# Inverse softmax sums spread by a VectorE block transpose and two DMAs through DRAM instead of GpSimd, TensorE and ScalarE

## Chip, cores and metric

One NeuronCore of a Trainium2 chip runs the whole program. The metric is the device time of one execution in microseconds (us). The kernel before takes 1790.45 us (median of three runs, 1790.11 to 1791.4).

## What is computed

Input and output are 2 x 2048 tokens of 256 features, fp32. The first part is an attention with 16 heads of 16 and an MLP; the second is two layers, each a local attention with 8 heads of 64 and a gated MLP. The change is in the attention of these two layers, called B here:

```python
w = n // WINDOW                                   # windows of 128 tokens
bk, bv = (look_around(bk), look_around(bv))       # keys and values of this window and the one before
sim = jnp.einsum('bhwid,bhwjd->bhwij', bq, bk)
sim = jnp.where(mask, -jnp.finfo(sim.dtype).max, sim)
attn = jax.nn.softmax(sim, axis=-1)
out = jnp.einsum('bhwij,bhwjd->bhwid', attn, bv)
...
x = x + o @ wo
```

The division of the softmax is done late: the kernel forms exp(sim - max) @ v without it and multiplies the result by 1 / sum, once per head and query.

## The kernel before

The tokens are cut into 32 chunks of 128 (`NCH`), a chunk being one window of one batch. A B attention is one loop of software-pipelined steps `s`, written out by hand for each engine. In step `s` TensorE does, in this order: `scores(s)` (L851, two rounds of four heads), `values(s-1)` (L890), `spread_inverse(s-1)` (L911), `project_k(s+2)`, `transpose_probs(s,0)` (L877), `project_q(s+2)`, `transpose_x(s+3)`, `transpose_probs(s,1)`, `transpose_rotated(s+1)`, `out_project(s-2)` (L923), `project_v(s+2)` (L830). Each engine runs its list in order and waits on semaphores; nothing is reordered.

VectorE does in step `s`: `maxima(s)` (L1330, eight masked maxima out of PSUM), `rotate_q(s+1)`, `scale_o(s-1)` (L1360, `O` times `b_inv_t`), `copy_probs(s,0)` (L1347, recorded at L1450), `scale_rotated(s+1)` (L1311), `norms(s+2,1)`, `copy_probs(s,1)`, `norms(s+2,0)` (L1286, with the small L1295), `invert_sums(s)` (L1354), `h_low(s+3)` (L1281), `k_t_low`, `q_t_low` (L1320, L1325), `add_residual(s-2)` (L1367). ScalarE does the exponentials (L1828, which also give `row_sum`), copies out of PSUM, among them `copy_spread(s-1)` (L1848) between its two rounds of exponentials. GpSimd does `o_low`, in the steps 5, 7, ... 19 a piece of splitting the MLP weights (L1138), `inverse_norms` (L2066), `tables` (L2045), `rotate_k(s+2)` (L2056), `widen_inverse(s)` (L2076). SyncE issues all DMAs (`sp_attention`, L388).

The sums stand with queries on partitions and heads on columns (`row_sum`, 128 x 8). The output `O` of `values` stands with features on partitions (two heads of 64 rows in each of four 128-column tiles) and queries on columns. So the inverse must be turned and repeated 64 times: VectorE inverts (128 x 8), GpSimd repeats each column 64 times (`b_inv_wide`, 128 x 512), TensorE turns four 128 x 128 blocks into PSUM bank W2 (bank 1), ScalarE copies W2 to `b_inv_t`, and VectorE multiplies.

Bank W2 has three users in a step: the spread, the transposed input (`transpose_x(s+3)`, read by ScalarE's `h_high` and VectorE's `h_low`) and `project_v(s+2)`, read by ScalarE's `copy_v`. `project_v(n)` waits at L836 for `h_lo` to have reached `min(n + 2, NCH)`, that is, for `h_low(s+3)` of the same step. The last chunks of an attention overlap the first groups of the MLP behind it: at `s == NCH - 2` SyncE issues that MLP's first loads (`sp_mlp(..., opening=True)`, L493), and at `s == NCH - 1` VectorE interleaves the MLP's normalisation with `scale_o(30)` and `invert_sums(31)`.

Of the kernel before, what the change touches and what calls it, by code (L numbers as in the profile page):

```python
# [6 lines left out]
F32 = mybir.dt.float32  # L7
# [6 lines left out]
P = 128  # L14
# [142 lines left out]
def build(nc, io):  # L157
# [5 lines left out]
    x_mid_sh = nc.dram_tensor("x_mid_sh", (TOK + P, P), F32, kind="Internal").ap()  # L163

    ctx = ExitStack()
    with ctx:
# [20 lines left out]
        minus_half = sbuf("minus_half", [P, 16])  # L187
        vec_a = sbuf("vec_a", [P, 16])
# [42 lines left out]
        b_inv, b_inv_wide = sbuf("b_inv", [P, 8], at=b_ctx), sbuf("b_inv_wide", [P, 512], at=b_ctx)  # L231
        b_inv_t = sbuf("b_inv_t", [P, 512], at=b_ctx)
# [64 lines left out]
        def sems(prefix, names):  # L297
# [11 lines left out]
            inv_ready inv_wide inv_spread r_copied o_scaled o_hi o_lo wo_ready y_ready""")  # L309
# [78 lines left out]
        def sp_attention(sp, layer, opening=False):  # L388

            S, g0 = SB, layer * NCH  # L390
# [385 lines left out]
        def pe_attention(pe, layer, opening=False):  # L776
# [10 lines left out]
            def transpose_x(n):  # L787
# [7 lines left out]
                if n > 3:  # L795
                    pe.wait_ge(S["v_copied"], g0 + n - 1)
                    pe.wait_ge(S["r_copied"], g0 + n - 3)
# [32 lines left out]
            def project_v(n):  # L830
# [6 lines left out]
                if n >= 3:  # L837
                    pe.wait_ge(S["r_copied"], g0 + n - 2)
# [72 lines left out]
            def spread_inverse(n):  # L911

                pe.wait_ge(S["inv_wide"], g0 + n + 1)
                pe.wait_ge(S["v_copied"], g0 + min(n + 3, NCH))
                if n == NCH - 2:
                    pe.wait_ge(S["y_ready"], g0 + NCH - 3)
                if n == NCH - 1:
                    pe.wait_ge(S["r_copied"], g0 + n)
# [33 lines left out]
            for s in b_steps():  # L952
# [320 lines left out]
        def dve_attention(v, layer, opening=False):  # L1273
# [80 lines left out]
            def invert_sums(n):  # L1354
                v.wait_ge(S["exp_ready"], 2 * (g0 + n) + 2)
# [960 lines left out]
```

## Time and profile before

| | us |
|---|---|
| median of three runs | 1790.45 |
| profiled execution, first to last instruction | 1791.1 |
| of it, first B attention (571 to 978) | 407 |
| second B attention (1180 to 1592) | 412 |

The page of the profile gives for the whole span: TensorE busy 97%, VectorE 83%, ScalarE 67%, GpSimd 60%; the DMA queue that SyncE fills takes 20.5% of 16 engines' time. In the views, times are microseconds from the start of the span; PE is TensorE (matmul), PEld its weight loads, DVE VectorE, ACT ScalarE, POOL GpSimd, SPq SyncE's DMA issues. A number in square brackets at the end of a row is idle time of the engine before that instruction, with what ended it. Where a row has xN, it joins N instructions of one kind.

### The profile page before, as it was taken

How to read it: one execution, taken by the hardware profiler on the slowest of the kernel's cores; microseconds unless marked ns; L12 is line 12 of the kernel's file. 1: busy time of each engine (PE TensorE's matmuls, PEld its weight loads, DVE VectorE, ACT ScalarE, POOL GpSimd, SP SyncE). 2: the span in 40 equal slices, each digit the busy share in tenths (PEclk: the TensorE clock that was granted, in tenths of full speed). 3: DMA queues.
4: the chain of work that ended last, by engine and by line, in shares of the span. 5: the costliest groups of instructions: out<-in, count | busy, mean ns of one | idle time of the engine just before them, and what ended most of it. 6: DMA issues, size and time to landing. Idle time of an engine off the chain costs nothing.

```text
span 1791.1 us, 43798 instructions
## 1 busy us (share of the span) xinstructions
PE 1731.2 (97%) x15424; PEld 1496.0 (84%) x15424; DVE 1494.1 (83%) x3797; ACT 1197.5 (67%) x3088; POOL 1080.0 (60%) x1060
## 2 busy tenths in 40 slices
PE   6999999999999999999999999989999999999997
PEld 4778777789998888888887888878888888888886
DVE  6888988868878898888987678789898898967776
ACT  6999988854445787877876334358787877743332
POOL 3676556534434778778773455377878777634343
PEclk9999999999999999999999999999999999999999
DMA  3111211032322111111112434331111111131221
GB/s 107 38 37 38 67 44 31 26 107 75 108 63 99 48 41 54 44 52 51 44 43 71 147 105 126 100 103 41 52 44 55 41 54 47 31 102 56 82 82 36
DMA packets 139812, 116.03 MB, mean 65 GB/s; under 512 B 10584, under 2 KB 138848, under 8 KB 138848
## 3 DMA queue, kind: packets, MB, share of 16 engines
q1 hardware_dynamic: 139616, 113.53, 20.5%
q8 instruction: 109, 1.79, 0.4%
q14 instruction: 87, 0.71, 0.1%
HBM read 75.74 MB, written 37.75 MB: 63 GB/s over the span
## 4 chain that ended last, share of the span: by engine, by line
PE 84%; DVE 9%; ACT 3%; issue 3%; POOL 0%; DMA 0%; SPq 0%; DVEq 0%; POOLq 0%; ACTq 0%
PE psum L567 17%; PE psum L569 17%; PE psum L568 17%; PE psum L906 6%; PE psum L874 5%; PE psum L887 5%; PE psum L682 3%; PE psum L664 3%; PE psum L848 3%; ACT a_probs L1718 2%; PE psum L920 2%; PE psum L617 1%; DVE a_neg_max L1211 1%; DVE psum L1209 1%; PE psum L654 1%
## 5 line engine op out<-in xcount | busy, mean ns | idle before, releaser
L1837 ACT ACTIVATE b_probs<-masked,neg_max 128x256 f32<-128x256 f32 (+1 forms) x512 | 250.6, 494 | 124.3 <-DVE neg_max L1343 124.3
L1343 DVE CUSTOM_DVE_ANT_0 masked<-psum,mask 128x256 f32<-128x256 f32 (+1 forms) x512 | 177.3, 412 | 75.9 <-PE psum L874 75.9
L567 PE MATMUL psum<-wa_hi,b_h_hi 128*128 128x512 f32 (+1 forms) x576 | 233.8, 406 | 6.9 <-DVE wa_lo L1138 3.9
L568 PE MATMUL psum<-wa_lo,b_h_hi 128*128 128x512 f32 (+1 forms) x576 | 214.0, 372 | 0.0
L569 PE MATMUL psum<-wa_hi,b_h_lo 128*128 128x512 f32 (+1 forms) x576 | 214.0, 372 | 0.0
L567 PE MATMUL psum<-g_h_hi,wm_hi 128*128 128x512 f32 (+1 forms) x480 | 190.5, 397 | 2.7 <-POOL g_h_lo L2121 1.6
L2070 POOL TENSOR_TENSOR g_in<-g_in,minus_half 128x16 f32<-128x16 f32 x64 | 188.2, 2940 | 4.5 <-DVE g_in L1295 4.5
L568 PE MATMUL psum<-g_h_lo,wm_hi 128*128 128x512 f32 (+1 forms) x480 | 189.3, 394 | 0.0
L569 PE MATMUL psum<-g_h_hi,wm_lo 128*128 128x512 f32 (+1 forms) x480 | 189.2, 394 | 0.0
L1458 POOL TENSOR_TENSOR g_in<-g_z,g_in 128x512 f32<-128x512 f32 x62 | 79.8, 1287 | 143.4 <-DVE g_in L1289 138.2
L567 PE MATMUL psum<-wm_hi,u_hi 128*128 128x256 f32 x576 | 164.3, 285 | 0.1
L1931 ACT ACTIVATE gate<-psum,vec_b 128x512 f32<-128x512 f32 x96 | 66.1, 688 | 146.4 <-PE psum L569 146.3
L569 PE MATMUL psum<-wm_hi,u_lo 128*128 128x256 f32 x576 | 162.7, 283 | 0.0
L568 PE MATMUL psum<-wm_lo,u_hi 128*128 128x256 f32 x576 | 162.5, 282 | 0.0
L1718 ACT ACTIVATE a_probs<-psum,a_neg_max 128x128 f32<-128x128 f32 x512 | 148.5, 394 | 5.0 <-DVE a_neg_max L1211 4.9
L2008 POOL TENSOR_SCALAR_AFFINE_SELECT p_before<-p_now 128x512 f32<-128x512 f32 x120 | 76.6, 638 | 119.6 <-ACT p_now L1728 119.6
L887 PE MATMUL psum<-ident,b_probs 128*128 128x128 f32 x992 | 129.8, 273 | 3.7 <-ACT b_probs L1837 3.7
L569 PEld LDWEIGHTS psum<-wa_hi,b_h_lo 128*128 128x128 f32 x576 | 109.4, 190 | 19.9
L567 PEld LDWEIGHTS psum<-wa_hi,b_h_hi 128*128 128x128 f32 x576 | 109.7, 190 | 18.9 <-DVE wa_lo L1138 4.3
L887 PEld LDWEIGHTS psum<-ident,b_probs 128*128 128x128 f32 x992 | 113.0, 140 | 14.7 <-ACT b_probs L1837 6.7
L906 PE MATMUL psum<-b_pt,v_tok 128*64 128x128 f32 x1984 | 123.4, 277 | 0.0
L2117 POOL TENSOR_TENSOR g_rstd<-g_ve,minus_half 128x4 f32<-128x4 f32 x24 | 25.1, 1046 | 161.8 <-DVE g_ve L1487 161.8
(169 smaller groups left out, 5644.0 us busy)
## 6 DMA issues: line engine op xcount, KB each, us to landing
x_mid<-y_out SPq DMA_DIRECT2D x96, 128.0 KB, 1.7
rope_in<-in_rope SPq DMA_DIRECT2D x64, 128.0 KB, 2.2
x_res<-x_state SPq DMA_DIRECT2D x64, 128.0 KB, 2.2
g_in<-x_mid SPq DMA_DIRECT2D x32, 256.0 KB, 3.8
g_old<-x_state SPq DMA_DIRECT2D x16, 512.0 KB, 4.0
out_x<-g_fin SPq DMA_DIRECT2D x15, 512.0 KB, 2.9
w_raw<-in_w_mlp_b SPq DMA_DIRECT2D x2, 2154.0 KB, 8.8
x_in<-in_x SPq DMA_DIRECT2D x32, 128.0 KB, 2.2
```

What stands on the lines that cost most here:

```text
L567: nc.tensor.matmul(out, a_hi, b_hi, start=first, stop=False)
L568: nc.tensor.matmul(out, a_hi, b_lo, start=False, stop=False)
L569: return nc.tensor.matmul(out, a_lo, b_hi, start=False, stop=last)
L874: mm = nc.tensor.matmul(outs[b], q[rows, t, :], k[rows, t, at, :], start=first, stop=last)
L887: mm = nc.tensor.transpose(bank[4 + 2 * r + k // 2][:, at:at + P], b_probs[:, r, k, half, :], ident[:])
L906: mm = nc.tensor.matmul(O[rows, t * P:t * P + P], v_tok[m % U][:, h * 64:h * 64 + 64], b_pt[:, r, 2 * j + b, half, :], start=(m == blocks[ ...
L1343: ins = nc.vector.tensor_tensor_reduce(out[:, at], src[:, at], (mask if now else mask0)[:, at], -1.0, BIG, ALU.add, ALU.min, neg_max[:, r, ...
L1458: engine.tensor_tensor(cos_part[i][:].rearrange("p (h d) -> p h d", d=64), x, table(2 * i, 0, 64), ALU.mult).then_inc(done, 1)
L1718: ins = nc.scalar.activation(a_probs[:, i % 2, k, :], bank[4 + 2 * (i % 2) + b][:, at:at + P], ACT.Exp, bias=a_neg_max[:, n % 2, r, k:k + ...
L1837: ins = nc.scalar.activation(out, src, ACT.Exp, bias=neg_max[:, r, k:k + 1], scale=-1.0, accum_out=row_sum[:, n % 2, 4 * r + k:4 * r + k + 1])
L2008: nc.gpsimd.affine_select(before, now, [[0, 4], [-1, P]], ALU.is_ge, 0.0, base=-1, channel_multiplier=1)
L2070: nc.gpsimd.tensor_tensor(rnorm[:], norm2c[:], minus_half[:], ALU.pow).then_inc(S["rnorm_ready"], 1)
```

## The change

`spread_inverse`, `copy_spread` and `widen_inverse` go, with their semaphores and the waits on them. `b_inv` becomes 128 x 32, its columns 8 to 31 holding ones. VectorE, after the reciprocal, turns `b_inv` in 32 x 32 blocks into `b_inv_turned`: partition 32 g + h holds head h of the queries 32 g to 32 g + 31. SyncE stores that (128 rows of 128 bytes) to a DRAM tensor with heads on rows and 128 queries on columns, waits until it has landed, and issues two reads, each of which fills 64 partitions with the same four rows (256 pieces of 512 bytes each), into one half of a doubled `b_inv_t`. `scale_o` waits for these reads. `invert_sums(s)` moves forward in VectorE's order, from behind `norms(s+2,0)` to behind `scale_rotated(s+1)`. On SyncE the three DMAs of chunk `s` stand at the head of step `s`, ahead of the store of `y(s-2)`; in step 0 behind the last store of the layer before; in step 30 behind the first loads of the MLP.

```diff
@@ sp_attention
+            def inverse_of(n):
+                return inverse_rows[(n % 2) * 32:(n % 2) * 32 + 32, :]
+            def store_inverse(n):
+                sp.wait_ge(S["inv_turned"], g0 + n + 1)
+                if g0 + n >= 2:
+                    sp.wait_ge(S[f"inv_spread{n % 2}"], 32 * ((g0 + n) // 2))
+                sp.dma_start(inverse_of(n).rearrange("h (g q) -> g h q", q=32), b_inv_turned[:]).then_inc(S["inv_stored"], 16)
+            def spread_inverse(n):
+                sp.wait_ge(S["inv_stored"], 16 * (g0 + n + 1))
+                if g0 + n >= 2:
+                    sp.wait_ge(S["o_scaled"], g0 + n - 1)
+                for b in range(2):
+                    src = inverse_of(n)[0:c.NH, :].rearrange("(t b) q -> b t q", b=2)[b:b + 1, :, :].to_broadcast([c.DH, 4, P])
+                    sp.dma_start(b_inv_t[b * c.DH:(b + 1) * c.DH, n % 2, :, :], src).then_inc(S[f"inv_spread{n % 2}"], 16)
...
                 if s == NCH - 2:
                     sp_mlp(sp, MLP_B, MB, layer, opening=True)
+                if b_chunk(s) and s > 0:
+                    store_inverse(s)
+                    spread_inverse(s)
                 if b_chunk(s - 2):
                     store(s - 2)
...
                     sp_mlp(sp, *mlp_behind(layer), None if layer == 0 else layer - 1, opening="last")
+                    store_inverse(0)
+                    spread_inverse(0)
@@ pe_attention
                     pe.wait_ge(S["v_copied"], g0 + n - 1)
-                    pe.wait_ge(S["r_copied"], g0 + n - 3)
...
-                if n >= 3:
-                    pe.wait_ge(S["r_copied"], g0 + n - 2)
...
-            def spread_inverse(n):
-                pe.wait_ge(S["inv_wide"], g0 + n + 1)
-                pe.wait_ge(S["v_copied"], g0 + min(n + 3, NCH))
...
-                for t in range(4):
-                    mm = nc.tensor.transpose(W2[:, t * P:t * P + P], b_inv_wide[:, t * P:t * P + P], ident[:])
-                mm.then_inc(S["inv_spread"], 1)
...
-                    pe.wait_ge(S["r_copied"], g0 + NCH - 2)
+                    pe.wait_ge(S["v_copied"], g0 + NCH)
...
                     values(s - 1, 1)
-                    spread_inverse(s - 1)
@@ dve_attention
             def invert_sums(n):
                 v.wait_ge(S["exp_ready"], 2 * (g0 + n) + 2)
+                nc.vector.reciprocal(b_inv[:, 0:c.NH], row_sum[:, n % 2, :]).then_inc(S["inv_ready"], 1)
+                v.wait_ge(S["inv_ready"], g0 + n + 1)
                 if g0 + n > 0:
-                    v.wait_ge(S["inv_wide"], g0 + n)
-                nc.vector.reciprocal(b_inv[:], row_sum[:, n % 2, :]).then_inc(S["inv_ready"], 1)
+                    v.wait_ge(S["inv_stored"], 16 * (g0 + n))
+                nc.vector.transpose(b_inv_turned[:], b_inv[:]).then_inc(S["inv_turned"], 1)
 
             def scale_o(n):
-                v.wait_ge(S["r_copied"], g0 + n + 1)
+                v.wait_ge(S[f"inv_spread{n % 2}"], 32 * ((g0 + n) // 2) + 32)
...
                     scale_rotated(s + 1)
+                if b_chunk(s) and s != NCH - 1:
+                    invert_sums(s)
                 if s == NCH - 2:
                     add_residual(s - 2)
...
                     norms(s + 2, 0)
-                if b_chunk(s) and s != NCH - 1:
-                    invert_sums(s)
@@ act_attention
-            def copy_spread(n):
-                a.wait_ge(S["inv_spread"], g0 + n + 1)
-                if g0 + n > 0:
-                    a.wait_ge(S["o_scaled"], g0 + n)
-                nc.scalar.activation(b_inv_t[:], W2[:], ACT.Copy).then_inc(S["r_copied"], 1)
@@ pool_attention
-            def widen_inverse(n):
-                pool.wait_ge(S["inv_ready"], g0 + n + 1)
-                if n == 0:
-                    pool.wait_ge(zero_rows_stored, layer * 32 + 16)
...
-                nc.gpsimd.tensor_copy(b_inv_wide[:].rearrange("p (h d) -> p h d", d=64),
-                                      b_inv[:].unsqueeze(2).to_broadcast([P, 8, 64])).then_inc(S["inv_wide"], 1)
```

## Rows read from the trace of the kernel before

**Rows 1.** The page, part 4: the chain that ended last, by engine.

```profile
PE 84%; DVE 9%; ACT 3%; issue 3%; POOL 0%; DMA 0%; SPq 0%; DVEq 0%; POOLq 0%; ACTq 0%
```

**Rows 2.** Busy time by engine: a step with weights split, then a plain one.

```profile
core 0: us, PE busy (x) PEld busy (x) DVE busy (x) ACT busy (x) POOL busy (x), PEclk, DMA share, GB/s
684.59:697.20 12.61, 12.61 (x118) 11.14 (x118) 11.38 (x33) 9.91 (x28) 10.62 (x10) 1.00 0.16 49
722.42:735.01 12.59, 12.59 (x119) 11.12 (x118) 11.28 (x33) 10.45 (x29) 9.43 (x9) 1.00 0.15 48
```

**Rows 3.** The chain that ended last, in the plain step: start, length, engine, line.

```profile
725.96 0.59 PE psum L920 x4
```

**Rows 4.** Timeline, plain step, VectorE: start, length, line, operation, output<-input, shapes.

```profile
723.39 0.42 DVE L1343 CUSTOM_DVE_ANT_0 masked<-psum,mask 128x256 f32<-128x256 f32 x1 [1.17 <-PE psum L874]
...
728.15 0.68 DVE L1365 TENSOR_TENSOR b_o<-psum,b_inv_t 128x512 f32<-128x512 f32 x1
728.86 0.69 DVE L1450 COPY b_pt<-psum 128x512 f32<-128x512 f32 x1
729.46 1.28 DVE L1318 TENSOR_TENSOR g_in<-g_in 128x512 f32<-128x512 f32 x2
730.66 0.68 DVE L1289 TENSOR_REDUCE g_in<-k_sq 128x8 f32<-128x512 f32 x1
...
731.95 0.68 DVE L1289 TENSOR_REDUCE g_in<-q_sq 128x8 f32<-128x512 f32 x1
732.65 0.17 DVE L1295 TENSOR_SCALAR g_in<-g_in 128x16 f32<-128x16 f32 x1
732.75 0.19 DVE L1358 RECIPROCAL b_inv<-row_sum 128x8 f32<-128x8 f32 x1
732.86 0.37 DVE L1283 TENSOR_TENSOR b_h_lo<-psum,b_h_hi 128x256 fp32r<-128x256 f32 x1
```

**Rows 5.** Timeline, plain step, TensorE: first scores, V projection's load, next first scores.

```profile
722.37 0.39 PE L874 MATMUL psum<-k_t_hi,q_t_hi 64*128 64x256 f32 x2
...
733.34 0.19 PEld L567 LDWEIGHTS psum<-wa_hi,b_h_hi 128*128 128x128 f32 x1
...
734.94 0.39 PE L874 MATMUL psum<-k_t_hi,q_t_hi 64*128 64x256 f32 x2
```

**Rows 6.** Timeline, plain step, GpSimd: the K rotation's first product.

```profile
731.51 1.29 POOL L1458 TENSOR_TENSOR g_in<-g_z,g_in 128x512 f32<-128x512 f32 x1 [2.41 <-DVE g_in L1289]
```

**Rows 7.** Timeline, step with weights split: GpSimd, VectorE and TensorE's load.

```profile
691.10 0.75 POOL L2053 TENSOR_TENSOR g_in<-rope_in,rope_scale 128x256 f32<-128x256 f32 x1
...
691.61 1.39 DVE L1318 TENSOR_TENSOR g_in<-g_in 128x512 f32<-128x512 f32 x2
...
695.11 0.36 DVE L1283 TENSOR_TENSOR b_h_lo<-psum,b_h_hi 128x256 fp32r<-128x256 f32 x1
...
695.53 0.19 PEld L567 LDWEIGHTS psum<-wa_hi,b_h_hi 128*128 128x128 f32 x1
```

**Rows 8.** Timeline, VectorE, first chunk of the second batch.

```profile
778.69 0.42 DVE L1449 COPY b_pt<-psum 128x256 f32<-128x256 f32 x1 [0.51 <-PE psum L887]
```

**Rows 9.** The page, part 6: DMA issues, KB each, median us to landing.

```profile
x_mid_sh<-y_out SPq DMA_DIRECT2D x64, 64.0 KB, 1.7
g_in<-x_mid_sh SPq DMA_DIRECT2D x16, 256.0 KB, 3.5
```

**Rows 10.** Ends of both layers: SyncE's first y store and its landing, `scale_o(30)`.

```profile
960.90 0.75 SPq L405 DMA_DIRECT2D x_mid<-y_out  x1
DMA to landing us min/median/max: 1.7/1.7/3.8
...
965.55 0.68 DVE L1365 TENSOR_TENSOR b_o<-psum,b_inv_t 128x512 f32<-128x512 f32 x1
...
1570.38 0.50 SPq L405 DMA_DIRECT2D x_mid<-y_out  x1
...
1576.43 0.68 DVE L1365 TENSOR_TENSOR b_o<-psum,b_inv_t 128x512 f32<-128x512 f32 x1
```

**Rows 11.** Busy time, second layer, scores of chunk 31; PEclk is the granted clock.

```profile
1569.00:1572.00 3.00, 3.00 (x26) 2.78 (x28) 1.39 (x9) 0.00 (x0) 0.88 (x1) 0.50 0.94 248
```

More of the change, by code:

```diff
@@ L163, in build @@
     x_mid_sh = nc.dram_tensor("x_mid_sh", (TOK + P, P), F32, kind="Internal").ap()
+    inverse_rows = nc.dram_tensor("inverse_rows", (2 * 32, P), F32, kind="Internal").ap()
     ctx = ExitStack()
@@ L187, in build @@
         minus_half = sbuf("minus_half", [P, 16])
+        b_inv = sbuf("b_inv", [P, 32])
+        b_inv_turned = sbuf("b_inv_turned", [P, 32])
         vec_a = sbuf("vec_a", [P, 16])
@@ L230, in build @@
         row_sum = sbuf("row_sum", [P, 2, 8], at=b_ctx)
-        b_inv, b_inv_wide = sbuf("b_inv", [P, 8], at=b_ctx), sbuf("b_inv_wide", [P, 512], at=b_ctx)
-        b_inv_t = sbuf("b_inv_t", [P, 512], at=b_ctx)
+        b_inv_t = sbuf("b_inv_t", [P, 2, 4, P], at=b_ctx)
         b_o = sbuf("b_o", [P, 512], at=b_ctx)
@@ L308, in build @@
             scores_ready max_ready exp_ready pt_ready pt_act pt_dve pv_done
-            inv_ready inv_wide inv_spread r_copied o_scaled o_hi o_lo wo_ready y_ready""")
+            inv_ready inv_turned inv_stored inv_spread0 inv_spread1 o_scaled o_hi o_lo wo_ready y_ready""")
         mlp_names = """load0 load1 old0 old1 store out_store params stats aggr var rstd z_ready xt_ready h32_ready h_hi h_lo h_lo_pool
@@ L388, in sp_attention @@
         def sp_attention(sp, layer, opening=False):
-            S, g0 = SB, layer * NCH
+            c, S, g0 = ATT_B, SB, layer * NCH
             def load(n):
@@ L909, in values @@
                 mm.then_inc(S["pv_done"], 1)
-            def spread_inverse(n):
-                pe.wait_ge(S["inv_wide"], g0 + n + 1)
-                pe.wait_ge(S["v_copied"], g0 + min(n + 3, NCH))
[L915 to L918, printed above, removed]
-                for t in range(4):
-                    mm = nc.tensor.transpose(W2[:, t * P:t * P + P], b_inv_wide[:, t * P:t * P + P], ident[:])
-                mm.then_inc(S["inv_spread"], 1)
             def out_project(n):
                 if n == NCH - 4:
-                    pe.wait_ge(S["r_copied"], g0 + NCH - 2)
+                    pe.wait_ge(S["v_copied"], g0 + NCH)
                 elif n == NCH - 3:
@@ L1364, in scale_o @@
                     v.wait_ge(S["o_lo"], g0 + n)
-                nc.vector.tensor_tensor(b_o[:], O[:], b_inv_t[:], ALU.mult).then_inc(S["o_scaled"], 1)
+                nc.vector.tensor_tensor(b_o[:].rearrange("p (t q) -> p t q", q=P), O[:].rearrange("p (t q) -> p t q", q=P),
+                                        b_inv_t[:, n % 2, :, :], ALU.mult).then_inc(S["o_scaled"], 1)
             def add_residual(n):
@@ L1647, in _ @@
             nc.vector.memset(big[:], -MASKED)
+            nc.vector.memset(b_inv[:], 1.0)
             nc.vector.memset(minus_half[:], -0.5).then_inc(consts_set, 1)
@@ L1880, in act_attention @@
                     exponentials(s, 0)
-                if b_chunk(s - 1):
-                    copy_spread(s - 1)
                 if b_chunk(s):
@@ L2074, in o_low @@
                 nc.gpsimd.tensor_tensor(b_o_lo[:], b_o[:], b_o_hi[:].bitcast(F32), ALU.subtract).then_inc(S["o_lo"], 1)
-            def widen_inverse(n):
-                pool.wait_ge(S["inv_ready"], g0 + n + 1)
-                if n == 0:
-                    pool.wait_ge(zero_rows_stored, layer * 32 + 16)
-                if g0 + n > 0:
-                    pool.wait_ge(S["inv_spread"], g0 + n)
-                nc.gpsimd.tensor_copy(b_inv_wide[:].rearrange("p (h d) -> p h d", d=64),
-                                      b_inv[:].unsqueeze(2).to_broadcast([P, 8, 64])).then_inc(S["inv_wide"], 1)
             if opening:
@@ L2109, in pool_attention @@
                     rotate_k(s + 2)
-                if b_chunk(s):
-                    widen_inverse(s)
             pool.wait_ge(S["y_ready"], g0 + NCH)
```

## Prediction

> **What bounds the kernel now.** I read the chain that ended last first: 84% of it lies on TensorE and 9% on VectorE [rows 1]. The change only touches the two later attentions, so the next view is one step (one chunk of 128 tokens) of them. TensorE is busy for all of such a step, 12.61 us in a step in which GpSimd also splits weights and 12.59 us in one in which it doesn't (a plain step) [rows 2]. The four transposes that spread the inverse sums are a piece of 0.59 us of that chain [rows 3]. Taken alone this says: 0.59 us less per step, 64 times. But the chain shows only which engine was last, not how late the next one was. So I laid VectorE's order beside TensorE's in a plain step [rows 4, 5].
>
> The link that matters is bank W2. `project_v(s+2)` writes it and waits until VectorE's `h_low(s+3)` (L1283) has read it. In the plain step `h_low` ends at 732.86 + 0.37 = 733.23, and TensorE loads the first weights of `project_v` at 733.34 [rows 4, 5]: 0.11 us of slack. In the other kind `h_low` ends at 695.11 + 0.36 = 695.47 and the load comes at 695.53 [rows 7]: there TensorE waits for it already, and 0.06 us is the price of the handover. From that load to the next scores are 734.94 - 733.34 = 1.60 us, and from scores to the first maximum 723.39 - 722.37 = 1.02 us [rows 4, 5]. So there is a second ring, VectorE from the first maximum to `h_low`, then `project_v`, then scores, and it is as long as TensorE's own. The removed transposes aren't in it.
>
> **The change, part by part, inside that ring.** Removed from TensorE: 0.59 us. It would reach `project_v` 0.59 us sooner and find `h_low` not done; what hides the gain is that ring. ScalarE's copy of the spread and GpSimd's widening are gone from engines that the ring doesn't wait for, GpSimd in one place excepted (below); that frees them and moves nothing.
>
> What VectorE gains: it waits once for TensorE inside the ring. `scale_o` to the first `copy_probs` takes 728.86 - 728.15 = 0.71 us, while the same kind of operation passes on after 729.46 - 728.86 = 0.60 [rows 4]; 0.10 us goes away.
>
> What VectorE gets: the reciprocal now has a follower that waits for it. Before, it cost the pitch 732.86 - 732.75 = 0.11 us. Now it costs its full 0.19 us plus some 0.03 for the handover to itself (L1289, 0.68 us from 731.95, has its dependant at 732.65, 0.02 after its end) [rows 4]: 0.22 us. The 32x32 turn over 128x32 is in no row. Its pitch is bounded below by zero (wholly overlapped; a gain is excluded for the instruction itself) and above by that of a 128x256 operation, 0.29 us (0.37 us less the 0.08 that neighbours overlap). Nearest is the 128x8 reciprocal with 0.19; I take 0.21 us of duration, 0.13 of pitch. Sum 0.22 + 0.13 = 0.35 us, and 0.11 is taken from its old place: 0.24 net. Both now stand behind `scale_rotated`, ahead of `norms` and `copy_probs(s,1)`. They wait for ScalarE's exponentials, which are over before that; queued behind them are the norms, on which GpSimd's K rotation waits, the second copy, for which `values` has time until the next step, and `h_low`, which has none.
>
> One more link: VectorE's tiny L1295 begins at 732.65 and ends at 732.82, and GpSimd's K rotation ends at 731.51 + 1.29 = 732.80 [rows 4, 6]. The Trainium skill (SBUF — State Buffer, section "Who interferes with whom") says that a VectorE tensor_scalar in a two-port mode and a GpSimd instruction exclude each other for a whole instruction. By the row I take the moment as fixed at 2.09 us after the K norms start (730.66 to 732.75), since the rotation starts behind those norms; without such a tie it would be 2.01, and the plain steps would give 3.0 us less in all.
>
> Plain step: first maximum to K norms 730.66 - 723.39 = 7.27, less 0.10, plus 0.35 is 7.52; plus 2.09 and 0.37 gives 9.98 for the end of `h_low`; plus 0.06, 1.60 and 1.02 gives 12.66 us, against 734.94 - 722.37 = 12.57 now: +0.09. There are 19 such steps per layer: +3.4 us for two layers. Step with weights split: the same terms (-0.10, +0.24), and `scale_rotated` loses 0.11 (1.39 us for two against 1.28), because GpSimd's L2053 at 691.10, lasting 0.75, which overlaps it, comes earlier once the widening is gone [rows 4, 7]: +0.03, 7 per layer, +0.4 us. In the half-size step of the second batch's first chunk VectorE waits 0.51 us for TensorE [rows 8], and in the step of chunk 29 there is no `h_low` to wait for. The gain of each lies between nothing and 0.59; I count 0.45 (most of the wait shown) and 0.4, once per layer: -1.7 us in all. In the first step of a layer the scores of chunk 1 wait for VectorE's `q_t_low`, behind the pair: +0.24 twice, +0.5. Steady part: +2.6 us.
>
> **The round trip through DRAM.** The rows for SyncE's transfers give 1.7 us from issue to landing for 64 KB stored, and for loads in 512-byte rows up to 3.5 us [rows 9]. The new chain in a plain step: turned at 7.52 behind the first maximum, stored at about 9.4, two loads issued 0.5 apart, the second landed by 9.5 + 0.5 + 3.5 = 13.5. `scale_o` asks for it in the next step at 12.66 + 4.76 = 17.4 (728.15 - 723.39 = 4.76 into the step). 3.9 us of cover; hidden. SyncE's own queue: the y store, residual and x loads are pushed behind by three issues, which their next users, a step or more later, don't feel.
>
> Where the cover is gone is the end of a layer. There SyncE first issues the loads of the next MLP and only then this store: it would leave at about 960.90, where now a y store leaves that lands 3.8 us later [rows 10]. So 964.7, plus 0.1, 0.5 and 3.0 for the loads behind the MLP's is 968.3, while `scale_o(30)` stands at 965.55: about 2.7 us. In the second layer 1570.38 + 3.8 + 3.6 = 1577.8 against 1576.43: 1.4 us. VectorE's order behind it leads straight into the MLP's first chunk, so these are paid. The turn itself is in that stretch too (0.25 a layer), and chunk 31's trip is late by some 0.35. Ends: 2.7 + 1.4 + 0.5 + 0.7 = +5.3 us. The bound below is none (the transfers land in time), the one above twice that.
>
> The Trainium skill (SBUF — State Buffer, "The DMA setup-cost knee") puts a fixed 2 us on every transfer. By it alone the trip of chunk 30 would land at 965.5 and 1575.0, cost nothing, and the sum would be 4.1 us less; the row of a store issued in just that place, 3.8 us, speaks against it.
>
> Sum: 2.6 + 5.3 = +7.9 us. The profiled execution spans 1791.1 us and the median of the three timed runs is 1790.45, so the one may be put on the other: 1798.3 us.
>
> **Rivals.**
> - TensorE stays the bound (the other side). If `h_low` does not hold `project_v` back, every full step falls to 12.0 us: 58 times 0.59 is -34, with the ends +5: about 1762. It decides from the point where `h_low` ends at least 0.59 us ahead of TensorE; the rows show 0.11 and 0. For it speaks only TensorE's share. Chance 0.08.
> - The same ring, but the pair on VectorE costs almost nothing beyond the old reciprocal, or the end of the layer is covered. With 0 instead of 0.24 the 52 steps give 12 us less than forecast; half of that, or the ends at zero, puts it near 1792: no measurable change. Chance 0.23.
> - The ends cost more: TensorE idles longer, and its clock falls. In the second layer the granted clock was 0.50 for the three microseconds from 1569 [rows 11], after TensorE had waited for VectorE; two more such stretches cost about 1.3 us each, and a loaded queue may add 2 us per layer: 1806. A turn as dear as a 128x256 operation ends there too. Chance 0.17.
> - The trip is late in every step: it must take over 9.9 us from the turn to landing, and then each microsecond costs some 60 us. Against it speaks the cover of 3.9 us. Chance 0.04, 1850 and more.
> - Forecast, 1792 to 1804: 0.48. That the removed instructions stay is excluded by the diff.
>
> The range reaches down to a free turn and up to the third rival: 1787 to 1811. About 0.2% (3.6 us) is what a measurement of this kernel can tell from none. Slower 0.66, same 0.22, faster 0.12.
>
> **What would show it.** Right: plain steps of 12.6 to 12.7 us, with TensorE's busy time near 12.0 in them and its idle time ahead of `project_v`, released by L1283's line; `scale_o` waiting for a transfer only for chunk 30 (and slightly 31) of a layer. Wrong: steps of 12.0 to 12.3 (the ring is looser), a turn over 0.4 us, or `scale_o` waiting in each step.

## The result, and the profile after

The changed kernel takes 1807.91 us in the median of four runs (1807.04 to 1810.35), the kernel before 1790.93 beside it (1790.11 to 1791.54). The ratio is 1.0096, with a 95% interval of 1.0084 to 1.0107: 17 us slower. The forecast was 1798.3 us, +7.9 us. The direction and the range hold, but the cost is more than twice what was forecast.

The profiled execution of the changed kernel spans 1807.0 us, 15.9 more than that of before. Its page, busy time by engine and then the chain that ended last:

```profile
PE 1722.9 (95%) x15168; PEld 1475.8 (82%) x15168; DVE 1503.3 (83%) x3862; ACT 1170.2 (65%) x3024; POOL 1043.5 (58%) x996
...
PE 56%; DVE 30%; issue 8%; ACT 3%; DMA 2%; SPq 1%; DVEq 0%; POOL 0%; POOLq 0%; ACTq 0%
```

In [rows 1] the same line read TensorE 84% and VectorE 9%. TensorE was relieved, and a part of the chain went over to VectorE (9% to 30%). The plain step that answers [rows 2], from scores to scores (columns as there):

```profile
712.44:725.11 12.67, 12.45 (x113) 10.76 (x113) 11.41 (x34) 9.52 (x27) 10.11 (x9) 1.00 0.25 70
```

The step is 12.67 us long, as forecast (12.66), and TensorE is now idle for 0.22 us of it. VectorE's timeline over the same kind of step answers [rows 4]:

```profile
718.22 0.68 DVE L1378 TENSOR_TENSOR b_o<-psum,b_inv_t 128x512 f32<-128x512 f32 x1
718.82 0.68 DVE L1464 COPY b_pt<-psum 128x512 f32<-128x512 f32 x1
719.41 1.28 DVE L1329 TENSOR_TENSOR g_in<-g_in 128x512 f32<-128x512 f32 x2
720.62 0.19 DVE L1367 RECIPROCAL b_inv<-row_sum 128x8 f32<-128x8 f32 x1
720.84 0.21 DVE L1371 STREAM_TRANSPOSE b_inv_turned<-b_inv 128x32 f32<-128x32 f32 x1
720.98 0.64 DVE L1300 TENSOR_REDUCE g_in<-k_sq 128x8 f32<-128x512 f32 x1
...
722.85 0.26 DVE L1306 TENSOR_SCALAR g_in<-g_in 128x16 f32<-128x16 f32 x1
723.03 0.41 DVE L1294 TENSOR_TENSOR b_h_lo<-psum,b_h_hi 128x256 fp32r<-128x256 f32 x1
...
724.56 0.41 DVE L1385 TENSOR_TENSOR y_out<-psum,x_res 128x256 f32<-128x256 f32 x1
726.12 0.42 DVE L1354 CUSTOM_DVE_ANT_0 masked<-psum,mask 128x256 f32<-128x256 f32 x1 [1.16 <-PE psum L898]
```

Three of the forecast's prices can be read here. The turn lasts 0.21 us (0.21 was taken). The reciprocal and the turn (the pair, in what follows) together move VectorE on by 720.98 - 720.62 = 0.36 us (0.35 was taken). The scaling passes on to the copy after 0.60 us, so the 0.10 us of waiting are gone. TensorE in the same step, answering [rows 5]:

```profile
723.49 0.50 PE L594 MATMUL psum<-wa_hi,b_h_hi 128*128 128x512 f32 x1 [0.22 <-DVE b_h_lo L1294]
...
725.11 0.39 PE L898 MATMUL psum<-k_t_hi,q_t_hi 64*128 64x256 f32 x2
```

**Where the 15.9 us lie.** Both kernels scale the values once per chunk (L1365 before, L1378 after), so its 64 starts mark the same point of the work in each. The differences after - before of the times between these starts are:

| stretch | before, us | after, us | difference | forecast |
|---|---|---|---|---|
| layer 1, up to chunk 1 | 602.17 | 604.14 | +1.97 | +0.25 |
| layer 1, chunks 2 to 29 | 352.05 | 353.42 | +1.37 | +1.05 |
| layer 1, chunks 30 and 31 | 18.14 | 23.94 | +5.80 | 3.3 |
| between, up to layer 2's chunk 1 | 239.61 | 239.68 | +0.07 | +0.25 |
| layer 2, chunks 2 to 29 | 351.72 | 353.51 | +1.79 | +1.05 |
| layer 2, chunks 30 and 31 | 19.30 | 24.66 | +5.36 | 2.0 |
| behind it | 208.11 | 207.65 | -0.46 | 0 |

So the steady steps cost about what was said (3.2 us against 2.1 for these chunks). The surprise is at the ends: 11.2 us against 5.3. The start of the first layer adds 1.7 us more. Here is the end of layer 1 in the changed kernel, first VectorE and SyncE's queue (SPq):

```profile
960.19 0.21 DVE L1371 STREAM_TRANSPOSE b_inv_turned<-b_inv 128x32 f32<-128x32 f32 x1
...
963.70 0.51 SPq L494 DMA_DIRECT2D g_in<-x_mid  x1
964.31 0.57 SPq L433 DMA_DIRECT2D inverse_rows<-b_inv_turned  x1
968.90 1.26 SPq L442 DMA_DIRECT2D b_inv_t<-inverse_rows  x2
...
972.66 0.69 DVE L1378 TENSOR_TENSOR b_o<-psum,b_inv_t 128x512 f32<-128x512 f32 x1 [3.69 <-DMA b_inv_t<-inverse_rows]
973.27 2.32 DVE L1506 TENSOR_SCALAR g_z<-g_in,g_mv,g_rstd 128x256 f32<-128x256 f32 x4
975.51 0.19 DVE L1367 RECIPROCAL b_inv<-row_sum 128x8 f32<-128x8 f32 x1
...
981.50 0.69 DVE L1378 TENSOR_TENSOR b_o<-psum,b_inv_t 128x512 f32<-128x512 f32 x1 [0.37 <-DMA b_inv_t<-inverse_rows]
```

Chunk 30's inverses are turned at 960.40, but SyncE is issuing the MLP's loads until 964.2. The store goes out at 964.31, and the reads that wait for its landing are issued 4.6 us later. Its answering row in [rows 10] was 965.55. Behind the scaling that waits stand g_z (the normalised input of the MLP) and the turn of chunk 31, so chunk 31's trip starts only at 975.9. In layer 2 the wait is as long (3.87 us at 1589.97), but the kernel before itself is 1.4 us slower there than in layer 1 (12.74 us up to chunk 30 against 11.33), with the clock at 0.50 for a stretch [rows 11]; the changed kernel's execution has the clock at 1.00 there, so the difference of that end, +5.36, comes out smaller by that much. TensorE and the granted clock (PEclk, third number from the end of a window) in that place:

```profile
975.74 1.94 PE L1035 MATMUL psum<-ident,g_z 128*128 128x128 f32 x8 [5.21 <-DVE g_z L1506]
...
971.00:974.00 3.00, 0.00 (x0) 0.00 (x0) 1.34 (x4) 0.77 (x2) 0.00 (x0) 1.00 0.56 168
974.00:977.00 3.00, 1.26 (x6) 1.29 (x7) 2.97 (x6) 0.02 (x1) 1.34 (x1) 0.60 0.00 0
977.00:980.00 3.00, 3.00 (x26) 2.67 (x26) 1.64 (x3) 0.65 (x1) 0.00 (x0) 0.50 0.16 42
```

TensorE idles for 5.21 us, and the clock falls to the lower of its two levels (1.2 of 2.4 GHz) when it starts again.

### The profile page after: what moved, and what is told of

Its sections match the earlier page's. It is cut to its first block, busy times and chain, and to the rows that moved or that the text cites. A ratio compares the mean times of both kernels' runs of the same rounds, so it can differ in the third digit from the quotient of the medians.

```text
span 1807.0 us, 43288 instructions
## 1 busy us (share of the span) xinstructions
PE 1722.9 (95%) x15168; PEld 1475.8 (82%) x15168; DVE 1503.3 (83%) x3862; ACT 1170.2 (65%) x3024; POOL 1043.5 (58%) x996
## 4 chain that ended last, share of the span: by engine, by line
PE 56%; DVE 30%; issue 8%; ACT 3%; DMA 2%; SPq 1%; DVEq 0%; POOL 0%; POOLq 0%; ACTq 0%
PE psum L594 14%; PE psum L596 13%; PE psum L595 13%; DVE masked L1354 7%; DVE g_in L1329 4%; PE psum L709 3%; PE psum L898 3%; PE psum L691 3%; DVE b_pt L1464 3%; DVE g_in L1300 2%; ACT a_probs L1733 2%; DVE g_in L1472 2%; PE psum L644 1%; DVE a_neg_max L1222 1%; DVE psum L1220 1%
## 5 line engine op out<-in xcount | busy, mean ns | idle before, releaser
L594 PE MATMUL psum<-wa_hi,b_h_hi 128*128 128x512 f32 (+1 forms) x576 | 239.9, 416 | 19.1 <-DVE b_h_lo L1294 14.7
L595 PEld LDWEIGHTS psum<-wa_lo,b_h_hi 128*128 128x128 f32 x576 | 110.4, 192 | 11.0
```

What stands on the lines that cost most here:

```text
L594: nc.tensor.matmul(out, a_hi, b_hi, start=first, stop=False)
L595: nc.tensor.matmul(out, a_hi, b_lo, start=False, stop=False)
```

## The experiments

For each run these numbers count: the ratio to the kernel before on the same chip, and from the trace of one execution the plain step and the two ends (chunks 30 and 31 together, layer 1 / layer 2), both as times between starts of the scaling. The kernels of the rows "no turn", "before, no transposes" and "chunk 30 without its wait" leave out a part of the work (the turn, the transposes, chunk 30's inverses), to price it.

| kernel | median, us | ratio and 95% interval | plain step | ends |
|---|---|---|---|---|
| before | 1790.93 | 1 | 12.57, 12.63 | 18.14 / 19.30 |
| changed | 1807.91 | 1.0096 (1.0084 to 1.0107) | 12.67 | 23.94 / 24.66 |
| TensorE's transposes back | 1814.04 | 1.0138 (1.0121 to 1.0154) | 12.80 | 24.19 / 24.33 |
| turn behind h_low | 1806.17 | 1.0095 (1.0078 to 1.0112) | 12.68 | 25.02 / 25.10 |
| MLP loads behind | 1804.22 | 1.0080 (1.0063 to 1.0097) | 12.68 | 23.17 / 23.09 |
| no turn | 1791.73 | 1.0003 (0.9993 to 1.0012) | 12.42 | 24.21 / 24.58 |
| before, no transposes | 1789.06 | 0.9987 (0.9977 to 0.9996) | 12.57 | 18.14 / 18.23 |
| norms behind | 1790.63 | 0.9991 (0.9982 to 1.0001) | 12.36, 12.44 | 24.52 / 25.01 |
| before, norms behind | 1786.35 | 0.9974 (0.9965 to 0.9984) | 12.57 | 18.14 / 19.29 |
| chunk 30 without its wait | 1797.12 | 1.0031 (1.0021 to 1.0041) | 12.68 | 20.52 / 20.57 |
| TensorE kept busy | 1805.49 | 1.0074 (1.0056 to 1.0091) | 12.68 | 25.13 / 25.65 |
| g_z first | 1799.88 | 1.0047 (1.0030 to 1.0064) | 12.68 | 20.40 / 20.37 |
| ends mended | 1797.56 | 1.0033 (1.0020 to 1.0046) | 12.68 | 19.80 / 20.10 |
| all of it | 1777.53 | 0.9922 (0.9905 to 0.9938) | 12.36, 12.44 | 19.75 / 19.91 |

**TensorE's transposes put back.** Does TensorE's time count in a step?

```
# TensorE, behind values(s - 1), chunks 0 to 28
+ pe.wait_ge(S["v_copied"], g0 + n + 3)
+ for t in range(4):
+     nc.tensor.transpose(W2[:, t * P:t * P + P], ident[:], ident[:])
```

> The changed kernel, with TensorE given its four transposes of each of chunks 0 to 28 back (58 chunks in all, four 128x128 transposes into bank W2 behind the values, of data that nothing uses); nobody waits for their result but the next projection into the bank, on TensorE itself. Theory of the ring (VectorE's first maximum, h_low, the projection of the values, the scores): in a steady step TensorE waits for h_low longer than these 0.59 us last, so the time stays at that of the changed kernel, 1807 to 1809 us. Rival, that TensorE's own time sets a step: 58 x 0.59 = 34 us more, about 1842 us.

The result lies between the two: 12.80 us a step, +0.13 and neither 0 nor +0.59. The rival falls, and the ring as I had it (nobody waits for these transposes) is not whole either. The trace shows where most of the 0.13 goes in. VectorE's first copy of probabilities follows the scaling after 0.71 us here and after 0.60 in the changed kernel. The transposes of probabilities that it reads stand behind the four added ones on TensorE:

```profile
717.04 0.69 DVE L1385 TENSOR_TENSOR b_o<-psum,b_inv_t 128x512 f32<-128x512 f32 x1
717.75 0.69 DVE L1471 COPY b_pt<-psum 128x512 f32<-128x512 f32 x1
```

**The turn moved behind h_low.** By my ring the pair leaves the path.

```
# VectorE
- invert_sums(s)            # behind scale_rotated
  ...
  h_low(s + 3)
+ invert_sums(s)
  k_t_low(s + 1)
```

> The changed kernel, with VectorE's reciprocal and turn of a step moved from ahead of h_low to behind it (ahead of k_t_low). Ring: the two instructions (0.36 us by their start-to-start times in the trace) leave the chain that holds a step, about 52 steady steps are shorter by up to that, at most 18.7 us less, near 1789 us; the steady step falls from 12.67 to about 12.31 us. What could eat it: the values in DRAM are stored later by half a us, and scale_o then waits for its DMA, which gives a part back. Rival, that VectorE's order does not matter: 1808 us and a step of 12.67 us.

The step stayed at 12.68 us, so the ring ending in `h_low` fell as the thing that alone sets the step. TensorE's `project_v` no longer waits, but now the scores do (TensorE and VectorE of this run):

```profile
722.13 0.42 DVE L1385 TENSOR_TENSOR y_out<-psum,x_res 128x256 f32<-128x256 f32 x1
...
722.69 0.39 PE L898 MATMUL psum<-k_t_hi,q_t_hi 64*128 64x256 f32 x2 [0.28 <-DVE y_out L1385]
...
723.71 0.42 DVE L1354 CUSTOM_DVE_ANT_0 masked<-psum,mask 128x256 f32<-128x256 f32 x1 [1.16 <-PE psum L898]
```

The scores wait (`y_ready`, in the kernel's code) for the residual sum `y_out`, the last thing that VectorE does in a step, since they write the bank that it reads. From its start to the scores are 0.56 us here. In the changed kernel it is 725.11 - 724.56 = 0.55, and in the kernel before 722.37 [rows 5] less the 721.81 of this row of before:

```profile
721.81 0.41 DVE L1371 TENSOR_TENSOR y_out<-psum,x_res 128x256 f32<-128x256 f32 x1
```

That is 0.56 again. So all of VectorE's order lies in the ring: first maximum, everything up to `y_out`, the scores, and again the first maximum, with VectorE's only idle time, 1.16 us, at the handover. It makes no difference where in that order an instruction stands. My arm over `h_low` and `project_v` is as long to within 0.1 us, which is why its number was right: with the pair's 0.36 us taken out of it, TensorE is idle for 0.28 us ahead of the scores, and with the pair in it, in the changed kernel, for none.

**The turn left out.**

```
# VectorE, in invert_sums
- nc.vector.transpose(b_inv_turned[:], b_inv[:])
# SyncE, in store_inverse
- sp.wait_ge(S["inv_turned"], g0 + n + 1)
+ sp.wait_ge(S["inv_ready"], g0 + n + 1)
```

> The changed kernel without VectorE's turn of 32x32 blocks: the store reads a buffer that holds ones, so the output is not scaled by the inverse sums, and all else is as it was. Prices the turn alone: by the ring about 0.21 to 0.24 us less in each of 52 steady steps, 11 to 12.5 us less in all and some more at the ends, 1794 to 1797 us; the steady step falls from 12.67 to 12.43 us. Rival, that VectorE has the time free: 1807 us.

The step is 12.42 us (12.43 said), the time 1791.73 us, 2 us below what was expected, and the reciprocal passes on after 0.11 us where it was 0.36:

```profile
717.55 0.20 DVE L1367 RECIPROCAL b_inv<-row_sum 128x8 f32<-128x8 f32 x1
717.66 0.64 DVE L1300 TENSOR_REDUCE g_in<-k_sq 128x8 f32<-128x512 f32 x1
```

The turn costs 0.25 us a step, 13 us in 52 steps, of the 16.7 us between the ratios 1.0096 and 1.0003: 0.14 of it is its own (720.84 to 720.98), and 0.11 the reciprocal's, which now has a follower that waits for it. In the changed kernel most of these 13 us don't show as a loss, because VectorE was relieved elsewhere in the step (0.10 us of waiting at the copy, and 0.11 in `scale_rotated` in the steps in which GpSimd splits weights). Without the turn that relief pays for the dearer ends, and the time is that of the kernel before. Taken together with the run before: moving the turn brings nothing, leaving it out brings its full price. That is the mark of a ring that holds a whole engine.

**The kernel before without TensorE's transposes.** The same question there.

```
# TensorE, in spread_inverse
- for t in range(4):
-     mm = nc.tensor.transpose(W2[:, t * P:t * P + P], b_inv_wide[:, t * P:t * P + P], ident[:])
- mm.then_inc(S["inv_spread"], 1)
+ pe.sem_inc(S["inv_spread"], 1)
# ScalarE
- nc.scalar.activation(b_inv_t[:], W2[:], ACT.Copy)
+ nc.scalar.activation(b_inv_t[:], b_inv_wide[:], ACT.Copy)
```

> The kernel before, without TensorE's four transposes of the repeated inverses (ScalarE copies the block in SBUF, not turned; the scaling uses wrong factors). The run with VectorE's turn moved showed that the step did not care where on VectorE it stood, and in both kernels the scores start 0.56 us after the residual sum starts. Theory of VectorE's whole line: all of VectorE's work of a step, and the 1.16 us from its last instruction over the scores to the first maximum, hold a step, in the kernel before too; there a copy of probabilities waits some 0.09 us for TensorE, and that alone goes: 50 steps x 0.09 to 0.12 = 5 to 6 us less, 1785 to 1787 us. Rival, that the kernel before is held by TensorE's stream: 58 x 0.59 = 34 us less, 1757 us.

It gives 2.3 us less by the ratio, and the steps are 12.57 us throughout, where before they were 12.57 and 12.63. It is the direction of the whole line, at half its size. The rival (1757) is out: TensorE's stream alone did not hold the kernel before, although the chain of waits put 84% on it.

**VectorE's Q norms moved into its idle time.** If the whole line is the ring, the cure is to fill the 1.16 us.

```
# VectorE
- norms(s + 2, 0)           # ahead of h_low
  ...
  add_residual(s - 2)
+ norms(s + 2, 0)
```

> The changed kernel, with VectorE's sum of squares of Q and the clamp behind it (0.60 + 0.27 us in the trace) moved from ahead of h_low to behind the residual sum, into the 1.16 us in which VectorE waits for the scores. Theory of the whole line: the step falls by up to 0.86 us until TensorE holds it; TensorE's own instructions of a step are 12.57 - 0.59 = 11.98 us and small waits of 0.1 to 0.2: 12.0 to 12.2 us a step, 52 x 0.47 to 0.67 = 24 to 35 us less, 1773 to 1784 us. Rival, that GpSimd's reciprocal root (2.9 us) comes late by it and its wait takes the place: 1800 to 1808 us.

> The same move in the kernel before. Theory: VectorE is relieved here too, but TensorE's instructions fill 12.57 us of a step of 12.58 to 12.63, so almost nothing comes of it: 0 to 5 us less, 1786 to 1791 us. The difference to the changed kernel with the same move is what TensorE's 0.59 us are worth once VectorE does not hold the step. Rival, that VectorE alone held it: 24 to 35 us less, as in the changed kernel.

In the changed kernel the step falls from 12.67 to 12.36 and 12.44 us, and the time by 1.0096 - 0.9991, 19 us. In the kernel before it stays at 12.57, and the 4.7 us less in all lie in the trace mostly in the stretches up to each layer's chunk 1 (2.1 us each). So both engines held the kernel before at one length, TensorE at 12.57 (this run) and VectorE at 12.57 (the run without transposes). The direction is as expected for both, but the first missed its size for two reasons. VectorE's clamp, 0.26 us long in the changed kernel, takes 1.09 here, until GpSimd's K rotation ends (722.05 + 1.32 = 723.37), and the first maximum is held until then:

```profile
722.05 1.32 POOL L2071 TENSOR_TENSOR g_in<-g_in,k_sq 128x512 f32<-128x512 f32 x1
...
722.31 1.09 DVE L1306 TENSOR_SCALAR g_in<-g_in 128x16 f32<-128x16 f32 x1
723.31 0.41 DVE L1354 CUSTOM_DVE_ANT_0 masked<-psum,mask 128x256 f32<-128x256 f32 x1
```

The Trainium skill (SBUF — State Buffer, "Who interferes with whom") calls the port pair that VectorE and GpSimd share an exclusive lock. By that rule a clamp that starts under a GpSimd instruction is held until that one ends, and these rows agree (the clamp ends at 723.40). The second reason is that TensorE's floor is not 11.98 us. By starts, the four transposes hold up the next projection in the kernel before by 0.41 us, not 0.59, which was the length of a piece up to its modelled end [rows 3]:

```profile
725.89 0.66 PE L920 MATMUL psum<-ident,b_inv_wide 128*128 128x128 f32 x4
726.30 0.48 PE L567 MATMUL psum<-wa_hi,b_h_hi 128*128 128x512 f32 x1
```

The floor without the transposes is then 12.57 - 0.41 = 12.16 us. No run takes the two reasons apart.

**The ends: SyncE's order.**

```
# SyncE, s == NCH - 2
- sp_mlp(sp, MLP_B, MB, layer, opening=True)
  store_inverse(s); spread_inverse(s)
+ sp_mlp(sp, MLP_B, MB, layer, opening=True)
```

> The changed kernel, with SyncE's opening loads of the next MLP issued behind the store and the reads of chunk 30's inverses, not ahead of them, in both layers. Theory of the ends: chunk 30's store waited 0.6 us to be issued and landed after 4.6 us because the loads were in the queues ahead of it; without them its trip is about 3 us shorter, and the clock falls less: 3 to 5 us less at each end, 1798 to 1801 us in all. Rival, that the loads then come late and their own wait takes its place, or that another wait holds the end: 1806 to 1808 us.

A third of it came: the ratio is 1.0080, 2.9 us less, and the trace has 2.3 of it at the ends, where 6 to 10 were expected. Chunk 30's trip is over in time, but now VectorE waits for the MLP's input, which is the rival:

```profile
970.67 1.40 DVE L1494 BATCH_NORM_STATS2 g_stats<-g_in 128x6 f32<-128x256 f32 x4 [3.35 <-DMA g_in<-x_mid]
```

Chunk 31 still comes late: 8.40 and 8.98 us after chunk 30, which here waits for nothing, against 6.81 and 6.56 in the kernel before.

**Chunk 30 without its wait.**

```
# VectorE, scale_o, n == NCH - 2
- v.wait_ge(S[f"inv_spread{n % 2}"], ...)
- in1 = b_inv_t[:, n % 2, :, :]
+ in1 = ident[:].unsqueeze(1).to_broadcast([P, 4, P])
```

> The changed kernel, where the scaling of chunk 30 in both layers takes a constant matrix (the identity, four times over) in place of the inverses and does not wait for their trip; the trip is made all the same. Prices that wait alone with what hangs on it. Theory, that the trip and the fall of TensorE's clock behind it make the ends dear: chunk 30 comes 3.7 and 2.5 us earlier, and the second half of the end, which runs at the lower clock, 1 to 2 us in each layer: 8 to 11 us less, 1797 to 1800 us. Rival, that only the wait counts and the clock falls anyway: 6 us less, 1802 us.

The ratio is 1.0031, 11.6 us below that of the changed kernel. In the trace the ends are 20.52 and 20.57 us, 3.4 and 4.1 shorter, and neither has a fall of the clock. What stays over the kernel before (+2.4 in layer 1) is chunk 31's own wait:

```profile
967.79 0.21 DVE L1371 STREAM_TRANSPOSE b_inv_turned<-b_inv 128x32 f32<-128x32 f32 x1
...
974.62 0.69 DVE L1385 TENSOR_TENSOR b_o<-psum,b_inv_t 128x512 f32<-128x512 f32 x1 [2.20 <-DMA b_inv_t<-inverse_rows]
```

From the end of the turn to the scaling are 974.62 - 968.00 = 6.6 us. The kernel before has far less room at this place; from the work behind its reciprocal to the scaling of chunk 31 are 4.6 us:

```profile
967.79 1.24 DVE L1450 COPY b_pt<-psum 128x512 f32<-128x512 f32 x2
...
972.36 0.68 DVE L1365 TENSOR_TENSOR b_o<-psum,b_inv_t 128x512 f32<-128x512 f32 x1
```

So chunk 31's trip is uncovered whether chunk 30 waits or not: chunk 31 comes 9.20 and 9.24 us after chunk 30 here, 8.84 and 9.38 in the changed kernel.

The ends explain 7.5 of the 11.6 us. The rest lies in other stretches. In the one profiled execution, 15.0 us shorter than that of the changed kernel, the MLP between the layers is 1.9 us shorter and the start 3.5; the clock fell at other places in the two, and I can't tie this to the edit.

**The clock.** Forty transposes of the identity on TensorE while it waits for g_z.

```
# TensorE, s == NCH - 1, ahead of the transposes of g_z
+ for t in range(40):
+     nc.tensor.transpose(bank[MLP_B.FIRST_Z[0]][:, t % 4 * P:t % 4 * P + P], ident[:], ident[:])
```

> The changed kernel, with 40 transposes of the identity added on TensorE at the end of each layer (into a bank that is written anew right behind them), in the 5.2 us in which TensorE waits there for g_z: about 40 x 0.11 = 4.4 us of work that nobody needs. Prices the fall of the granted clock that follows that wait (0.60 and 0.50 in the windows behind it, the transposes of g_z, the values and VectorE's g_z slower). Theory, that the idle wait brings the fall: the clock stays at 1.00 behind it, and 2 to 3 us of each end come back, 4 to 6 us less in all, 1802 to 1804 us. Rival, that the clock falls all the same, or that the transposes are in the way: 1807 to 1811 us.

In layer 1 the clock stayed at 1.00 where it was 0.60 and 0.50:

```profile
974.00:977.00 3.00, 2.33 (x32) 2.16 (x34) 2.97 (x7) 0.00 (x0) 0.47 (x1) 1.00 0.04 5
977.00:980.00 3.00, 2.28 (x25) 1.91 (x20) 1.27 (x2) 1.06 (x1) 1.24 (x1) 1.00 0.17 49
...
980.67 0.47 PE L594 MATMUL psum<-g_h_hi,wm_hi 128*128 128x512 f32 x1 [1.39 <-POOL g_h_lo L2119]
...
981.69 0.69 DVE L1380 TENSOR_TENSOR b_o<-psum,b_inv_t 128x512 f32<-128x512 f32 x1 [2.29 <-DMA b_inv_t<-inverse_rows]
```

From chunk 30's scaling to the MLP's first matmul are 980.67 - 971.68 = 8.99 us, against 982.82 - 972.66 = 10.16 in the changed kernel. In this pair of executions the fall costs 1.2 us up to that matmul, not 2 to 3. In layer 2 the clock still fell (to 0.69). By the ratios, 1.0074 against 1.0096, the run is 3.9 us faster (1805.49 us, 1802 to 1804 expected), but their intervals overlap, so the size is not settled. Chunk 31 gained nothing (10.01 us behind chunk 30 instead of 8.84): what stands ahead of it came earlier, its trip did not, and it waits 2.29 us for it instead of 0.37. SyncE took 2.17 us to issue its two reads instead of 1.26. The slow g_z was not the clock's doing either: it takes 2.33 us here too. The last of its four instructions lasts 1351 ns (tile g_z in the changed kernel) and runs while GpSimd makes `b_o_lo`:

```profile
974.10 1.34 POOL L2081 TENSOR_TENSOR b_o_lo<-b_o,b_o_hi 128x512 fp32r<-128x512 f32 x1 [4.40 <-ACT b_o_hi L1867]
...
L1506 DVE TENSOR_SCALAR g_z<-g_in,g_mv,g_rstd x4: 404/406/1351, 973.3 to 974.2; 128x256 f32<-128x256 f32 x4
```

In the run with the loads behind, GpSimd started at 975.50, behind the last of them, and g_z took 1.38 us.

**VectorE's order at the end, then SyncE's too, then all.**

```
# VectorE, s == NCH - 1
- scale_o(s - 1)
  dve_mlp(v, MLP_B, MB, layer, opening=1)      # g_z
  invert_sums(s)
+ scale_o(s - 1)
```

> The changed kernel, where VectorE in the last step of a layer makes g_z of the next MLP and turns chunk 31's inverses ahead of the scaling of chunk 30, which waits 3.7 us for its trip, not behind it. Theory: the wait then holds only the scaling itself; g_z, TensorE's transposes of it and chunk 31's trip start 3 to 4 us earlier, and TensorE's wait is shorter, so the clock falls less: 3 to 5 us less at each end, 1797 to 1801 us. Rival, that the end is set by the scaling of chunk 30 and what follows it on TensorE (values, output projection) whatever VectorE does before it: 1806 to 1808 us.

1799.88 us, as expected: 8.8 us by the ratios, 3.5 and 4.3 at the two ends. The wait for chunk 30 is 1.42 us instead of 3.69, and chunk 31 waits for nothing:

```profile
971.19 0.69 DVE L1378 TENSOR_TENSOR b_o<-psum,b_inv_t 128x512 f32<-128x512 f32 x1 [1.42 <-DMA b_inv_t<-inverse_rows]
...
976.26 0.69 DVE L1378 TENSOR_TENSOR b_o<-psum,b_inv_t 128x512 f32<-128x512 f32 x1
```

```
# SyncE, s == NCH - 2
  load(0, 0)
+ store_inverse(s)
  loads of vec_b and row_b2
+ spread_inverse(s)
  load(1, 1)
# SyncE, s == 0
+ store_inverse(0)
  sp_mlp(..., opening="last")
  spread_inverse(0)
```

> The last one, and SyncE's order mended too: the store of chunk 30's inverses right behind the first MLP group's loads, their reads behind the two parameter loads, the second group's loads last; and chunk 0's store ahead of the last stores of the MLP before. Theory: chunk 30's trip is 2 to 3 us shorter in each layer and the start of a layer 1 to 2: 1792 to 1797 us. Rival, that shorter trips move nothing once g_z goes first: as the last run.

Another 2.5 us by the ratios. The ends are 19.80 and 20.10 us, 1.7 and 0.8 over the kernel before. The start of layer 1 did not improve. Chunk 0's scaling no longer waits for its trip (588.41 in the row below, without a wait), but chunk 1's follows after 14.15 us, as in the changed kernel: the clock falls between them in both (here 0.81 and 0.62 in the windows from 592 and 595).

```profile
588.41 0.69 DVE L1396 TENSOR_TENSOR b_o<-psum,b_inv_t 128x512 f32<-128x512 f32 x1
```

The time ends just above what was expected.

> The last one with VectorE's sum of squares and clamp moved behind the residual sum as well (steady step 12.36 to 12.45 us there): 1790.6 us of that run alone less what the mended ends give, 10 us or so: 1777 to 1783 us, 8 to 14 us less than the kernel before and 3 to 9 less than the kernel before with the same move. Rival, that the ends' gain and the step's overlap: 1784 to 1788 us.

1777.53 us, as expected: 14 us (0.8%) faster than the kernel before and 9 faster than the kernel before with the norms moved (0.9974 - 0.9922 of 1791). The ends are still no shorter than before (19.75 and 19.91 us), so this comes from the steps, 12.36 instead of 12.57 us. So the change is worth having, once VectorE and the ends are put in order for it. The mended orders at the ends were not tried in the kernel before.

## Why the prediction was right and wrong

- **VectorE's line is as long as TensorE's, and TensorE's relief buys next to nothing.** Right, and now shown: without TensorE's transposes the kernel before gained 2 us, not 34, and its step stayed at 12.57. The first rival (1762) is out.
- **The ring over `h_low` and `project_v`.** Right in its value (12.66 said, 12.67 measured), wrong as a mechanism. The step is held by VectorE's whole order up to `y_out`, then the scores' bank. Within the forecast this error cost nothing, since both arms contain the pair and are of one length; that was luck. It would have misled anyone who moved the pair behind `h_low`: 18.7 us were expected of that, and none came.
- **The pair's price,** 0.35 us said, 0.36 measured; the turn 0.21 and 0.21. The split holds too: by starts, the reciprocal passes on after 0.22 us and the turn after 0.14 (0.22 and 0.13 said). Leaving the turn out saves 0.25, since the reciprocal then has no follower that waits for it.
- **TensorE's 0.59 us.** A step that nothing in the sum hung on but a bound of the half-size steps, and wrong: 0.41 by starts. The criterion "TensorE's busy time near 12.0" failed with it (12.45 in the window, modelled ends included).
- **The steady part,** 2.6 us said with 0.5 for the first steps. Chunks 2 to 29 gave +1.4 and +1.8, 1.1 more than their share. The half-size steps gave back 0.5 in layer 1 (11.55 and 13.01 us became 11.51 and 12.72; chunk 29, 12.54 became 12.34) where 0.85 was counted.
- **The ends: the step that failed,** 5.3 us said, 11.2 measured. The term that failed is "chunk 31's trip is late by some 0.35": +2.0 and +2.8 us measured, 4.2 of the 5.9 us that the ends are off. No row stood behind the 0.35, and the prediction's own figures speak against it. They give a trip 13.5 - 7.52 = 6.0 us, and the kernel before has 4.6 us between the place of the turn and the scaling of chunk 31, so 1.4 us were uncovered by them. The run without chunk 30's wait shows the term alone, with the clock at 1.00: chunk 31 waits 2.20 us for its trip and comes 2.4 and 2.7 us later after chunk 30 than before. In the changed kernel the same lateness has several parts (layer 1 / layer 2): the slow g_z ahead of the turn 0.7 / 1.0, the pair 0.25 / 0.25, VectorE's next wait for TensorE's transposes of g_z, which run at the lower clock, 0.6 / 0.6, and what is left of the trip 0.45 / 1.0. With g_z and the turn put first, it goes (5.07 us from chunk 30 to 31), because the turn then stands ahead of chunk 30's scaling (969.55 and 971.19).
- **Chunk 30** was mis-sized too, by less: 2.7 and 1.4 said, with the turn 2.95 and 1.65, and +3.8 and +2.5 measured. From the store's issue to the scaling 7.4 us were said (960.90 to 968.3), and 8.35 measured (964.31 to 972.66): 4.6 to the reads instead of 3.9, 3.8 from there instead of 3.5.
- **The start of the first layer,** 0.25 said, +1.97 measured. Chunk 0's scaling waits 0.99 us for its trip, whose two reads took 2.28 us to issue. I had looked for uncovered trips only at the ends. But up to chunk 0 only 0.20 us are lost. The other 1.77 lie between chunks 0 and 1, where the clock falls (0.62 and 0.81 in the windows from 595 and 598) and VectorE waits 2.99 us for the scores. That the trip brings this fall is not shown: with the ends mended chunk 0 waits for nothing and the clock falls all the same (14.15 us), and without the turn it waits 1.39 us and the clock stays at 1.00 behind it (12.38 us, as the 12.37 before).

```profile
585.34 2.28 SPq L442 DMA_DIRECT2D b_inv_t<-inverse_rows  x2
...
590.00 0.69 DVE L1378 TENSOR_TENSOR b_o<-psum,b_inv_t 128x512 f32<-128x512 f32 x1 [0.99 <-DMA b_inv_t<-inverse_rows]
...
599.38 0.42 DVE L1354 CUSTOM_DVE_ANT_0 masked<-psum,mask 128x256 f32<-128x256 f32 x1 [2.99 <-PE psum L898]
```

- **The third rival** (the ends dearer, the clock falls: 1806, chance 0.17) is what happened, though its reasons were only partly right, so that its number was in part luck: the clock's part is 1.2 us in the one end where it could be read, the loaded queue added 1.0 to chunk 30's trip (8.35 against 7.4) where up to 2 was allowed, and the turn was not dear. What it lacks is chunk 31's uncovered trip, which VectorE's new order takes away (3.5 and 4.3 us less at the two ends).
- **The trip is hidden in steady steps.** Right: in all, the scaling waited for a transfer 5 times of 64. In the plain step the turn ends at 721.05, the second read lands at about 726.6, and the scaling starts at 730.89.

Open: which part of the differences between single executions is the clock falling in places that no edit touches, and why the fall at chunk 1 of layer 1 came in some kernels and not in others. Open too is why SyncE now and then takes 2.2 us to issue the two reads (2.28 for chunk 0, 2.17 in the run with TensorE kept busy) and otherwise 1.26.

## What to carry to other kernels

Where a chain puts nearly all on one engine, add up the next engine's order over one period, with the handover that closes it. If it reaches the period, relief of the first engine is worth next to nothing, and what counts of an added instruction is what it moves the second engine on by (start to start), wherever it stands. Test it in a pair: move the instruction, and leave it out. When a result begins to travel through DRAM, look at every place where the order of queues is not the steady one. There, compare the trip with the room that each such place leaves it, by rows, and look at what stands in order behind the instruction that waits: put that work first, the start of the next trip above all.

## What was not expected of the hardware

- A VectorE instruction that starts under GpSimd's work can be held until that ends: the 128x16 clamp took 1.09 us instead of 0.26, and a 128x256 tensor_scalar of g_z 1.35 us instead of 0.41.
- The granted clock fell to 0.50 for some us near the start of layer 1 in some kernels and not in others, and whether an instruction waited there for its transfer did not decide it.
- A 16 KB store behind queued loads let its reads go 4.6 us after its issue, while in steady steps it was 2.0 (721.08 to 723.08).
- Four 128x128 transposes take 0.41 us of TensorE's line, start to start, where the chain of waits shows a piece of 0.59.
